# Matrix-memory attention heads in a decoder stack: denominators moved to another place in the quad, a third output tile, and running distances that keep their mask in PSUM

## The reference

```python
lf = concatenate([0, cumsum(log_sigmoid(f_pre))])
log_d = lf[..., 1:, None] - lf[..., None, 1:] + i_pre[..., None, :]
log_d = where(t >= s, log_d, -inf)
m = max(log_d, axis=-1)
d_mat = exp(log_d - m)
s_mat = (q @ k.T / sqrt(32)) * d_mat
denom = maximum(abs(sum(s_mat, -1)), exp(-m)) + 5e-5
h = s_mat @ v / denom
```

## Time and profile before

| | |
|---|---|
| median of 3 runs | 3021.46 us (3018.62 to 3022.26) |
| the profiled execution | 3021.09 us, span of its trace 3019.4 us |
| busy over the span: TensorE, VectorE, ScalarE, GpSimd | 89%, 70%, 60%, 25% |
| `mlstm_gates`, `mlstm_heads` in the trace | from 363.8 us, from 418.3 us to 752.0 us |

### The profile page before, as it was taken

How to read it: one execution, slowest core, us unless ns; L and a number is a source line. 1 busy time by engine, 2 the same in 40 slices (tenths; PEclk the granted TensorE clock), 3 DMA queues, 4 the chain that set the end, 5 groups by cost and what they waited for, 6 DMA issues and landing times. The chain is left out here.

```text
span 3019.4 us, 57693 instructions
## 1 busy us (share of the span) xinstructions
PE 2686.9 (89%) x20790; PEld 2002.4 (66%) x20807; DVE 2105.2 (70%) x3830; ACT 1815.0 (60%) x3003; POOL 743.2 (25%) x717
## 2 busy tenths in 40 slices
PE   8999889997888799999969999968898988849899
PEld 6777654553777688888957888845555555525587
DVE  5666648888332232111149999969999999979899
ACT  3333357786222122222247787759999999969886
POOL 0111104445455100010155555122122222020000
PEclk9999989998798899999979999979999999979999
DMA  7000052221455544444421111011101111016676
GB/s 247 1 1 1 32 193 80 86 85 54 150 192 192 188 142 143 145 139 143 155 76 41 37 43 41 10 30 29 27 26 28 30 30 29 16 72 266 235 233 201
DMA packets 135669, 291.87 MB, mean 97 GB/s; under 512 B 21520, under 2 KB 58384, under 8 KB 130832
## 3 DMA queue, kind: packets, MB, share of 16 engines
q1 hardware_dynamic: 117360, 235.29, 23.9%
q0 software_dynamic: 18080, 53.50, 5.4%
HBM read 184.90 MB, written 103.81 MB: 96 GB/s over the span
## 5 line engine op out<-in xcount | busy, mean ns | idle before, releaser
L1331 ACT ACTIVATE cx_h<-bank,early_b 128x256 f32<-128x256 f32 (+1 forms) x288 | 117.6, 460 | 388.4 <-PE bank L1283 388.4
L2050 DVE TENSOR_SCALAR e_low<-bank 128x2048 f32<-128x2048 f32 x128 | 293.4, 2292 | 28.0 <-PE bank L1934 28.0
L1283 PE MATMUL bank<-cx_zT,cx_w 128*128 128x256 f32 (+1 forms) x1152 | 250.1, 371 | 2.1 <-DMA cx_w<-cw_dram 1.3
L1916 ACT ACTIVATE e_low<-e_low 128x2048 f32<-128x2048 f32 x128 | 244.9, 1913 | 4.1
L1294 PE MATMUL bank<-early_w,cx_h 128*128 x1088 | 246.6, 379 | 0.0
L1914 ACT ACTIVATE e_low<-e_low 128x2048 f32<-128x2048 f32 x128 | 243.6, 1903 | 0.0
L1283 PEld LDWEIGHTS bank<-cx_zT,cx_w 128*128 128x128 f32 x1152 | 212.0, 192 | 30.3 <-DMA cx_w<-cw_dram 1.7
L1294 PEld LDWEIGHTS bank<-early_w,cx_h 128*128 128x128 f32 x1088 | 201.2, 190 | 24.4
L1934 PE MATMUL bank<-e_qT,e_kT 32*128 32x256 f32 x2048 | 147.4, 401 | 66.9 <-DVE e_high L2051 66.1
L1346 DVE COPY cx_zT<-bank 128x512 f32<-128x512 f32 (+1 forms) x72 | 47.7, 662 | 202.7 <-PE bank L1274 202.7
L1354 DVE TENSOR_TENSOR cx_y<-bank,early_b 128x512 f32<-128x512 f32 (+1 forms) x72 | 47.7, 662 | 198.7 <-PE bank L1294 198.7
(11 more groups left out here) (392 smaller groups left out, 6740.8 us busy)
## 6 DMA issues: line engine op xcount, KB each, us to landing
cx_w<-cw_dram SPq DMA_DIRECT2D x72, 512.0 KB, 3.6
hidden<-fu_h SPq DMA_DIRECT2D x32, 1024.0 KB, 3.8
fd_h<-hidden SPq DMA_DIRECT2D x64, 512.0 KB, 4.2
cx_rows<-expert_rows SPq DMA_DIRECT2D x64, 256.0 KB, 3.5
slot_y<-cx_y POOLq DMA_DIRECT2D x64, 256.0 KB, 2.6
early_ctx_first<-ctxT_dram SPq DMA_DIRECT2D x32, 256.0 KB, 6.1
queries<-g_qT SPq DMA_DIRECT2D x32, 256.0 KB, 5.3
b_qT<-queries SPq DMA_DIRECT2D x32, 256.0 KB
```

Of the source, the lines that this page charges most:

```text
L1283: last = nc.tensor.matmul(H[k][f // 2][:, (f % 2) * GROUP_ROWS:(f % 2) * GROUP_ROWS + cols], w1[k][:, c, f * P:(f + 1) * P], zT[k][:, c, 0 ...
L1916: nc.scalar.activation(flat(low[n % RING][:]), flat(low[n % RING][:]), ACT.Exp, scale=-1.0).then_inc(low_ready, 1)
L2050: nc.vector.tensor_scalar(flat(low[n % RING][:]), HEADS4.rearrange("p r s -> p (r s)"), -1.0, 0.0, ALU.mult, ALU.max).then_inc(neg_ready, 1)
```

## The change

It has three parts, and one that they need.

1. *Distances.* With `fresh` false, L724 (which was L717) adds onto what the bank still holds (start=False) and the mask product (L726, which was L718) is left out. The table then holds the difference to the head two before, so that the sum in the bank becomes the next head's distances, with its mask kept. A distance is fresh only where the bank was overwritten or the group's rows changed: heads 2 and 3 of every even quad (`back` came between), and heads 0 and 1 of an item with j = 0. That leaves 24 x 2 + 8 x 4 = 80 of the 256 mask products.
2. *Denominators.* Five instructions of `norm` become `denominators`, called behind the even quad; `rden` gets two tiles. The odd quad keeps the sum of the squares and the two products.
3. *Output tiles.* `o` has three tiles in turn, and L679 waits for GpSimd's work on an item one further back.
4. In `mlstm_gates` four small VectorE instructions make the differences (`change`) ahead of the first copy into `minus`.

```diff
+            nc.vector.tensor_copy(change[:, :, 2:4], which[:, :, 2:4]).then_inc(rows_ready, 1)
+            nc.vector.tensor_copy(change[:, 0, 0:2], which[:, 0, 0:2]).then_inc(rows_ready, 1)
+            nc.vector.tensor_tensor(change[:, :, 4:HEADS], which[:, :, 4:HEADS], which[:, :, 2:HEADS - 2], ALU.subtract).then_inc(rows_ready, 1)
+            nc.vector.tensor_tensor(change[:, 1:LANES4, 0:2], which[:, 1:LANES4, 0:2], which[:, 0:LANES4 - 1, HEADS - 2:HEADS], ALU.subtract).then_inc(rows_ready, 1)
...
-        o = [place[:, (12 + 2 * k) * COLS:(14 + 2 * k) * COLS].rearrange("p (n x) -> p n x", n=TB) for k in range(2)]
+        o = [place[:, (12 + 2 * k) * COLS:(14 + 2 * k) * COLS].rearrange("p (n x) -> p n x", n=TB) for k in range(2)] + [sb("o2", [P, TB, COLS])]
+        rden = [sb(f"rden{k}", [P, TB, HEADS]) for k in range(2)]
...
             def back(b):
-                if b > 1:
-                    act.wait_ge(y_ready, b - 1)
+                if b > 2:
+                    act.wait_ge(y_ready, b - 2)
...
-                nc.tensor.matmul(out[:, 0:COLS], minus[:, j, h, :], top3[b // LANES4 % 2][:], start=True, stop=False)
-                nc.tensor.matmul(wide(out), t["identb"][:], t["maskneg"][:].rearrange("p (x y) -> p x y", x=2), start=False, stop=True).then_inc(dd_raw, 1)
+                fresh = not c and (r > 1 or j == 0)
+                last = nc.tensor.matmul(out[:, 0:COLS], minus[:, j, h, :], top3[b // LANES4 % 2][:], start=fresh, stop=not fresh, skip_group_check=not fresh)
+                if fresh:
+                    last = nc.tensor.matmul(wide(out), t["identb"][:], t["maskneg"][:].rearrange("p (x y) -> p x y", x=2), start=False, stop=True)
+                last.then_inc(dd_raw, 1)
...
-            def norm(b):
-                ch = Chain(dve, small, NORM, b)
+            def denominators(b):
+                ch = Chain(dve, small, 0, 0, NORM * b)
...
-                ch.did(nc.vector.reciprocal(rden[:], den[:])).see()
+                if b > 1:
+                    dve.wait_ge(scale_ready, b - 1)
+                ch.did(nc.vector.reciprocal(rden[b % 2][:], den[:]))
+
+            def norm(b):
+                ch = Chain(dve, small, 0, 0, NORM * b + 5)
+                ch.see()
                 dve.wait_ge(sq_ready, b + 1)
...
+                if not c and 0 <= b - 2 < B:
+                    denominators(b - 2)
```

More of the change, by code:

```diff
@@ L418, in mlstm_gates @@
         low, high, heads, lane = sb("low", [P, 2 + 2 * HEADS]), sb("high", [P, 2 + 2 * HEADS]), sb("heads", [P, HEADS]), sb("lane", [P, LANES4])
-        which = sb("which", [P, LANES4, HEADS])
+        which, change = sb("which", [P, LANES4, HEADS]), sb("change", [P, LANES4, HEADS])
         z = [sb(f"z{j}", [P, TB, D]) for j in LANES]
@@ L507, in _ @@
                 if g < LANES4:
-                    nc.vector.tensor_copy(s["minus"][:, g], which[:, g, :, None].to_broadcast([P, HEADS, P]))
+                    nc.vector.tensor_copy(s["minus"][:, g], change[:, g, :, None].to_broadcast([P, HEADS, P]))
         @block.tensor
@@ L590, in mlstm_heads @@
         oT = sb("oT", [P, 3, S])
-        o = [place[:, (12 + 2 * k) * COLS:(14 + 2 * k) * COLS].rearrange("p (n x) -> p n x", n=TB) for k in range(2)]
+        o = [place[:, (12 + 2 * k) * COLS:(14 + 2 * k) * COLS].rearrange("p (n x) -> p n x", n=TB) for k in range(2)] + [sb("o2", [P, TB, COLS])]
         sq, y, yg = (sb(n, [P, TB, D]) for n in ("sq", "y", "yg"))
-        den, neg, rden, rden2, ss, rms, scale = (sb(n, [P, TB, HEADS]) for n in ("den", "neg", "rden", "rden2", "ss", "rms", "scale"))
+        den, neg, rden2, ss, rms, scale = (sb(n, [P, TB, HEADS]) for n in ("den", "neg", "rden2", "ss", "rms", "scale"))
+        rden = [sb(f"rden{k}", [P, TB, HEADS]) for k in range(2)]
         names = ("soft0", "soft", "chain", "top3", "gT_raw", "gT", "mT", "em0", "em", "c_free", "dd", "decay", "sc", "sm", "pv", "oT", "bt", "o",
@@ L623, in _ @@
                         pool.wait_ge(q_in, b)
-                    nc.gpsimd.tensor_tensor(sq[:], o[b % 2][:, :, 0:D], o[b % 2][:, :, 0:D], ALU.mult).then_inc(sq_ready, 1)
+                    nc.gpsimd.tensor_tensor(sq[:], o[b % 3][:, :, 0:D], o[b % 3][:, :, 0:D], ALU.mult).then_inc(sq_ready, 1)
                 if b:
@@ L627, in _ @@
                     pool.wait_ge(scale_ready, b)
-                    nc.gpsimd.tensor_tensor(heads_of(y[:]), heads_of(o[(b - 1) % 2][:, :, 0:D]), scale[:, :, :, None].to_broadcast([P, TB, HEADS, HD]), ALU.mult).then_inc(y_ready, 1)
+                    nc.gpsimd.tensor_tensor(heads_of(y[:]), heads_of(o[(b - 1) % 3][:, :, 0:D]), scale[:, :, :, None].to_broadcast([P, TB, HEADS, HD]), ALU.mult).then_inc(y_ready, 1)
                     pool.wait_ge(y_ready, b)
@@ L674, in back @@
             def back(b):
-                if b > 1:
-                    act.wait_ge(y_ready, b - 1)
+                if b > 2:
+                    act.wait_ge(y_ready, b - 2)
                 for n in range(TB):
                     act.wait_ge(bt_raw, 2 * b + n + 1)
-                    nc.scalar.activation(o[b % 2][:, n, :], DD[n][:, 0:COLS], ACT.Copy).then_inc(o_ready, 1)
+                    nc.scalar.activation(o[b % 3][:, n, :], DD[n][:, 0:COLS], ACT.Copy).then_inc(o_ready, 1)
             def root(b):
@@ L833, in weigh @@
                     nc.vector.scalar_tensor_tensor(sm[q % 2][r][:], SC[r][:, 0:COLS], float(HD) ** -0.5, decay[r][:], ALU.mult, ALU.mult).then_inc(sm_ready, 1)
-            def norm(b):
-                ch = Chain(dve, small, NORM, b)
+            def denominators(b):
+                ch = Chain(dve, small, 0, 0, NORM * b)
                 j, g = b % LANES4, b // LANES4
                 dve.wait_ge(o_ready, 2 * (b + 1))
-                ch.did(nc.vector.tensor_scalar(by_c(den[:]), dens_of(o[b % 2]), 5e-5, None, ALU.add))
-                ch.did(nc.vector.tensor_scalar(by_c(neg[:]), dens_of(o[b % 2]), -1.0, 5e-5, ALU.mult, ALU.add)).see()
+                ch.did(nc.vector.tensor_scalar(by_c(den[:]), dens_of(o[b % 3]), 5e-5, None, ALU.add))
+                ch.did(nc.vector.tensor_scalar(by_c(neg[:]), dens_of(o[b % 3]), -1.0, 5e-5, ALU.mult, ALU.add)).see()
                 ch.did(nc.vector.tensor_tensor(den[:], den[:], neg[:], ALU.max)).see()
@@ L843, in norm @@
                 ch.did(nc.vector.tensor_tensor(den[:], den[:], em[g % 2][:, :, j, :], ALU.max)).see()
-                ch.did(nc.vector.reciprocal(rden[:], den[:])).see()
+                if b > 1:
[4 more added lines that the diff above has]
+                ch.see()
                 dve.wait_ge(sq_ready, b + 1)
                 ch.did(nc.vector.tensor_reduce(ss[:], heads_of(sq[:]), AX.X, ALU.add))
-                ch.did(nc.vector.tensor_tensor(rden2[:], rden[:], rden[:], ALU.mult)).see()
-                ch.end()
+                ch.did(nc.vector.tensor_tensor(rden2[:], rden[b % 2][:], rden[b % 2][:], ALU.mult)).see()
                 if b:
@@ L869, in _ @@
                         dve.wait_ge(y_ready, b - 3)
-                    nc.vector.tensor_tensor(scale[:], rms[:], rden[:], ALU.mult).then_inc(scale_ready, 1)
+                    nc.vector.tensor_tensor(scale[:], rms[:], rden[(b - 3) % 2][:], ALU.mult).then_inc(scale_ready, 1)
                 if c and 0 <= b - 2 < B:
```

1 line of the change is left out of this document (added).

## The result

| | before | after |
|---|---|---|
| median of 5 runs each | 3021.98 us (3018.62 to 3024.76) | 3034.07 us (3029.81 to 3035.97) |
| the profiled execution, its span | 3021.09, 3019.4 us | 3032.76, 3031.0 us |
| mean granted clock of TensorE | 0.957 | 0.955 |
| first distance to last product into X | 326.1 us | 333.9 us |

The ratio is 1.0035 [1.0023, 1.0047]: slower by 12 us, where 3017 and a range up to 3026 were forecast. The change of the trace lies in three places. The first distance comes 1.1 us later (427.0 for 425.9). The heads take 7.9 us more. From the end of the heads to the experts' first large product (L1299) it is 261.0 us for 258.0.

A forecast was written before the change was run, and what follows sets the result against it. The order in which near-equally busy engines wait for each other was taken as the bound. Six middle groups -2.3 us, first and last together -2.4, gates +0.4: -4.3 on 3021.09, stated as 3017, range 3009 to 3026.

The forecast's parts named there:

- the second term: VectorE's chain at j = 1 and j = 2 with the moved denominators: 19.58 us, against 19.53 before.
- the tie: Third portion of `prepare` at j = 2: GpSimd's squares might start ahead of L819, which waits 1.04 us; 3024, chance 0.10.
- The sum: A middle group changes by -0.39 us, six by -2.3; with first and last groups and gates -4.3 us.
- The mask products: TensorE's list: 176 of 256 products go, 0.11 us each; 0.22 us less at j = 0 and at j = 3.
- The place of the stall that L862 inherits: Denominators: L847's successor meets the running L628 and takes over L841's stall, some 500 to 650 ns.
- L865 in its gap: VectorE: L851's successor starts in the 0.01 us between GpSimd's L628 and L630, as L843 did before.
- The gates: TensorE's wait for `g_z`: four small VectorE instructions delay the first copy into `minus`, +0.4 us, all on the path.
- The first and the last group: Without `norm` begun, or anything to prepare, j = 1 and j = 2 may gain; -1.2 us each, together -2.4.
- near the upper end: Choice of -1.2 us for each of the first and last groups, between -0.39 and -1.32.
- The third tile at nothing: Third output tile `o`: priced at nothing apart from j = 2, where VectorE's chain is the limit anyway.
- L851 misses its gap: Rival: L851 comes late and waits for L630's 1.29 us on VectorE; +12 us, 3029, chance 0.12.
- VectorE keeps up: Rival: at j = 1 and j = 2 VectorE isn't the limit; each group gains 1.32 us, 3011, chance 0.27.

The follow-up runs named there:

- sq_behind: Changed kernel, but in j = 0 items GpSimd's squares wait until the same item's denominators are done; ratio to before 1.0004, stage 324.6 us.
- den_only: Changed kernel with all 256 mask products back and two output tiles, denominators still behind the even quad; ratio to before 1.0019, stage 333.3 us.
- fillers: Changed kernel plus 28 useless bf16 matrix products in TensorE's wait ahead of the scores of every j = 3; ratio to before 1.0027, stage 332.5 us.
- third_late: Changed kernel with the third portion of `prepare` behind the odd quad of j = 2 instead of its even one; ratio to before 0.9987, stage 318.6 us.

## Why the prediction was wrong, point by point

*The step that failed* is the second term, the sum of VectorE's chain at j = 1 and j = 2: 19.58 us in the sum, 20.21 measured (9.62 + 10.59). Its parts were right: sq_behind, without the stall, has 9.62 + 9.80 = 19.42. What the sum left out is one stall, 0.78 us. The forecast had seen the tie and put it among the rivals at a chance of 0.10 and 1.04 us. Two steps there were mistaken. The first is the question "who wins?": it asked only for L819, and L819 won. The squares took 0.28 us longer and held L820's successor for 0.78. In this tie of long work on one engine with a list of short instructions on the other, the list loses either way; den_only and after show both ways, 0.59 with 0.3 for the later copy, or 0.78. The second is the time of the tie: at 4.01 against 4.02 us, both counted from the same instruction, the case deserved far more than a tenth. In six of seven groups it came. The Trainium skill's page "SBUF — State Buffer", section "Who interferes with whom", states more than the forecast took from it: `tensor_scalar`, `copy` and `cast`, when their operands let them use both ports for one tensor, can contend for the pair that GpSimd uses, not only instructions with two inputs. The trace agrees as to the wait, 1134 for 350 ns on L829, a `tensor_scalar` of one SBUF tensor; in which mode L829 ran no row says.

*What wasn't there at all* is the clock. Every term was taken at the full clock of the earlier trace rows. TensorE's wait ahead of j = 3 grew to 1.74 us, 0.50 was granted for about the first third of that item, and j = 3 took 10.51 and not 9.38. At 1.13 us or more in five groups it cost more than the stall, 0.78 in six. fillers (same stall, clock kept, j = 3 at 9.38) and sq_behind (both gone) show it.

*The sum:* a usual group was to gain 0.39 us and lost 1.37. The difference of 1.76 is 0.63 of the chain (20.21 for 19.58) and 1.13 of the clock (10.51 for 9.38). The six middle groups were to gain 2.3 us and lost 8.3 (232.7 before, 241.0 after).

*What was right.* The mask products: j = 0 took 9.35 and j = 3, at full clock, 9.38, both 0.22 less, and the block behind a distance without mask starts 0.26 us after it (the values at 528.79 behind L724 at 528.53). That j = 1 keeps nothing of its 0.44 (9.62 for 9.60), and nearly the length of VectorE's chain where no stall stands in it, 19.42 for 19.58. The place of the stall that L862 inherits, 646 ns in 500 to 650, and L865 in its gap. The gates, 0.43 for 0.4 at TensorE's wait for `g_z`.

*What was mis-sized.* The first and the last group were to gain 1.2 us each. The four steps of the first group gained 0.71 together; the last group with all behind it lost 0.3: its steps gained 0.1, and 0.4 went between the last even quad's scores and the end. The forecast took those "near the upper end" without a row for it. So even with stall and clock taken away, in sq_behind, the stage gains 1.5 us and not 4.7. Its first distance comes 1.4 us later than before's (1.0 of it ahead of the gates), and the ratio is 1.0004: no change. The third tile at nothing was nearly right, 0.11 per group.

*The rivals.* "L851 misses its gap" is refuted by 174/174/176. "VectorE keeps up" is refuted for this order, and what third_late does is that rival made true: with the portion elsewhere the four steps take 37.63, 1.07 less than before, where 1.32 were counted for it.

*Open:* why the clock stayed up in b = 23 of after behind the same wait, and behind 17 more waits of 1.49 us and over, so the wait alone doesn't decide it. Why single steps are up to 1.9 us longer than usual, at full clock too; many rows there name the load of `b_cn` as the releaser, and in three kernels the clock fell behind such a wait (1.61, 1.95 and 1.79 us). No run took those loads earlier.

## What to carry to other kernels

Where a long GpSimd instruction and a chain of short VectorE ones are released at nearly the same time, count the stall as paid, on the first or on the next, and either hold the long one until the chain is through or move the chain. An engine's saving in front of a wait only lengthens the wait, and on TensorE a longer wait can cost the clock of the item behind it: read the granted clock behind each of its long waits. When several short steps are to be fitted into one gap, try the places together: moving one portion by a quad turned the change's loss of 0.2 to 0.35% into a gain of 0.13%, and the same move with the denominators at their old place lost 0.4%.

## What the runs showed of the hardware

- In a tie with a long GpSimd instruction, the VectorE instruction kept its time (0.42 us) and GpSimd's squares took 1.32 us for 1.04. The next VectorE instruction of the list then took 0.66 to 0.78 us more, whether it was a `tensor_scalar` (1.13 for 0.35) or a `scalar_tensor_tensor` of 256 columns (1.14 for 0.48). When the squares started while one `scalar_tensor_tensor` ran, the one behind it, of 128 columns, took 1.13 for 0.35. With the squares 0.31 us ahead, they kept their 1.04 and the VectorE instruction took 1.01 for 0.42.
- The granted clock of TensorE fell to its lower level, 1.2 GHz, behind single waits of 1.5 to 2.1 us, in a stage that is at 1.00 otherwise: behind 25 of the 43 waits from 1.49 to 2.40 us in these traces, and behind none of the 22 from 1.0 to 1.43 us. The fall cost 1.13 us at j = 3, more than the stall of 0.78 that had lengthened the wait.
